# One transfer for ids and bounds, and the last quarter of the second layer's filters issued with the two quarters before it

## The reference

```python
e = stack([tbl_f[ids[:, f]] for f in range(32)], axis=1)          # b, 32, d

prev, outs = e, []
for W in (filter_0, filter_1):                                    # (1024, 128), (4096, 128)
    z = einsum('bhd,bmd->bhmd', e, prev)                          # every field times every map
    cur = relu(einsum('bpd,pn->bnd', z.reshape(b, h*m, d), W))
    outs.append(cur)
    prev = cur
z = concat(outs, axis=1).sum(-1)                                  # b, 256

h = relu(concat([z, dense_ctx], 1) @ W_top1 + b_top1)             # 512
h = relu(h @ W_top2 + b_top2)                                     # 256
y = h @ W_top3
```

## Time and profile before

| | |
|---|---|
| median of 3 runs | 844.33 us (843.94 to 844.5) |
| the profiled execution | 844.57 us |
| its span | 842.8 us |
| TensorE busy | 833.8 us, 99% of the span |
| VectorE, ScalarE, GpSimd busy | 803.8, 782.7, 726.4 us |
| granted TensorE clock | full in all but the very last slices |
| chain of work that ended last | TensorE 94% |

### The profile page before, as it was taken

How to read it: one execution, slowest core, us unless ns; L and a number is a source line. 1 busy time by engine, 2 the same in 40 slices (tenths; PEclk the granted TensorE clock), 3 DMA queues, 4 the chain that set the end, 5 groups by cost and what they waited for, 6 DMA issues and landing times.

```text
span 842.8 us, 17221 instructions
## 1 busy us (share of the span) xinstructions
PE 833.8 (99%) x3595; PEld 670.1 (80%) x3595; DVE 803.8 (95%) x877; ACT 782.7 (93%) x2779; POOL 726.4 (86%) x550
## 2 busy tenths in 40 slices
PE   8999999999999999999999999999999999999998
PEld 6687888888888888888888888888888888888777
DVE  7689999999999999999999999999999999999996
ACT  4799999999999999999999999999999999999984
POOL 5798888999888999888899888899888799988871
PEclk9999999999999999999999999999999999999999
DMA  4551233331232332132232123332123233112000
GB/s 147 166 155 40 56 83 81 83 84 51 43 85 78 82 85 67 29 82 78 83 84 78 30 69 79 83 83 84 41 53 82 79 84 84 47 48 76 1 13 1
DMA packets 62245, 60.17 MB, mean 71 GB/s; under 512 B 26347, under 2 KB 37227, under 8 KB 62222
## 3 DMA queue, kind: packets, MB, share of 16 engines
q1 hardware_dynamic: 58126, 57.80, 23.2%
q0 software_dynamic: 4096, 2.11, 3.3%
HBM read 55.51 MB, written 4.31 MB: 71 GB/s over the span
## 4 chain that ended last, share of the span: by engine, by line
PE 94%; DVE 2%; DMA 1%; POOL 1%; issue 1%; SPq 0%; ACT 0%; DVEq 0%
PE ps_y L895 27%; PE ps_y L903 27%; PE ps_y L896 27%; PE ps_c L868 3%; PE ps_c L878 3%; PE ps_c L877 2%; PE ps_c L876 2%; POOL gat L447 1%; DVE csum L737 1%; PE ps_c L874 1%; DVE prod L724 1%; DMA prod<-w 1%; DMA gat<-table,rows 0%; PE ps_y L999 0%; POOL w_lo L454 0%
## 5 line engine op out<-in xcount | busy, mean ns | idle before, releaser
L559 ACT ACTIVATE prod<-ps_y,es 128x128 f32<-128x128 f32 x2560 | 719.6, 490 | 37.3 <-PE ps_y L903 33.2
L737 DVE TENSOR_REDUCE csum<-prod 128x64 f32<-128x1664 f32 (+2 forms) x256 | 478.8, 1871 | 0.4 <-POOL prod L436 0.2
L895 PE MATMUL ps_y<-w_hi,c_both 128*128 128x512 f32 x1024 | 415.4, 406 | 2.9 <-POOL w_lo L454 2.1
L903 PE MATMUL ps_y<-w_hi,c_both 128*128 128x512 f32 x1024 | 399.6, 390 | 0.0
L896 PE MATMUL ps_y<-w_lo,c_both 128*128 128x512 f32 x1024 | 399.4, 390 | 0.0
L724 DVE TENSOR_TENSOR prod<-ps_y,es 128x512 f32<-128x512 f32 x384 | 256.3, 681 | 23.3 <-PE ps_y L903 17.0
L436 POOL TENSOR_TENSOR prod<-prod 128x768 f32<-128x768 f32 (+1 forms) x128 | 240.4, 1878 | 36.1 <-ACT prod L559 28.1
L895 PEld LDWEIGHTS ps_y<-w_hi,c_both 128*128 128x128 f32 x1024 | 192.4, 188 | 55.3 <-issue 11.5
L896 PEld LDWEIGHTS ps_y<-w_lo,c_both 128*128 128x128 f32 x1024 | 192.4, 188 | 48.2 <-issue 8.2
L903 PEld LDWEIGHTS ps_y<-w_hi,c_both 128*128 128x128 f32 x1024 | 192.2, 188 | 41.9
L426 POOL TENSOR_TENSOR z<-first,second 128x512 f32<-128x512 f32 x155 | 198.1, 1296 | 25.0 <-PE ps_c L874 24.9
(11 more groups left out here) (119 smaller groups left out, 290.0 us busy)
## 6 DMA issues: line engine op xcount, KB each, us to landing
second<-et_scratch SPq DMA_DIRECT2D x155, 256.0 KB, 3.6
first<-et_scratch SPq DMA_DIRECT2D x31, 256.0 KB, 3.3
et_scratch<-gat SPq DMA_DIRECT2D x62, 64.0 KB
prod<-w SPq DMA_DIRECT2D x4, 512.0 KB
h_scratch<-h_sums SPq DMA_DIRECT2D x120, 2.0 KB
gat<-table,rows_now POOLq DMA_INDIRECT x116
wt_sb<-wt SPq DMA_DIRECT2D x2, 512.0 KB
rows_now<-rows SPq DMA_DIRECT2D x30, 2.0 KB, 1.8
```

The lines of the kernel that those rows point to most:

```text
L559: last = nc.scalar.activation(prod[:, buffer_of(g, u), h // 2, :, h % 2], ps_y[:, bank_of(g, u, k), j * N:(j + 1) * N], ACT.Copy, scale=es ...
L737: nc.vector.tensor_reduce(csum[:, g.r, maps, u], prod[:, buffer_of(g, u), fields_folded(g, u) // 2:F // 2, maps, :].rearrange("p a n t -> ...
L895: nc.tensor.matmul(out, hi, w_hi, start=True, stop=False)
L903: nc.tensor.matmul(out, lo, w_hi, start=False, stop=True).then_inc(y_ready, 1)
```

## The change

Ids and bounds come in one array of 128 by 131 words (bounds as the bits of float32, read through a view), so one transfer takes the place of two, and VectorE waits for one. The three `sem_inc` of SyncE go behind quarter 0. Quarter 3 is issued with quarters 1 and 2, after the gathers of group 0, and no longer between `send` and `fetch`. ScalarE rounds bank 6 before bank (0, 1) instead of before (0, 3), and with it the z of the other tiles; bank 7 stays before (0, 3).

```diff
-        ids_sb = sb("ids_sb", [P, TILES], I32)
+        ids_and_bounds_sb = sb("ids_and_bounds_sb", [P, TILES + 3], I32)
-        bounds_sb = sb("bounds_sb", [P, 3])
+        ids_sb = ids_and_bounds_sb[:, 0:TILES]
+        bounds_sb = ids_and_bounds_sb[:, TILES:TILES + 3].bitcast(F32)
...
         def _(sp):
-            for s in range(SLOTS):
-                sp.sem_inc(h1_written[s], 16 * BT)
-            sp.dma_start(ids_sb[:, :], ids).then_inc(ids_in, 16)
-            sp.dma_start(bounds_sb[:, :], bounds).then_inc(ids_in, 16)
+            sp.dma_start(ids_and_bounds_sb[:, :], ids_and_bounds).then_inc(ids_in, 16)
...
             filters(0)
+            for s in range(SLOTS):
+                sp.sem_inc(h1_written[s], 16 * BT)
             sp.wait_ge(gathered[0], 16 * TG)
-            for n in range(1, W1_LOADS - 1):
+            for n in range(1, W1_LOADS):
                 filters(n)
...
             send(Group(0, 1))
-            filters(W1_LOADS - 1)
             fetch(Group(0, 1))
...
-                        if number == 0 and (u, k) == (0, 3):
+                        if number == 0 and (u, k) == (0, 1):
+                            round_w1((6,))
                             act.wait_ge(z_ready, KP)
                             round_z(slice(1, TG), z_hi_ready, SPLIT)
-                            round_w1((6, 7))
+                        if number == 0 and (u, k) == (0, 3):
+                            round_w1((7,))
...
-            dve.wait_ge(ids_in, 32)
+            dve.wait_ge(ids_in, 16)
```

More of the change, by code:

```diff
@@ L112, with tower @@
 LAST = Group((GROUPS - 1) // SLOTS, (GROUPS - 1) % SLOTS)
-def tower(nc, ids, bounds, copy_of, ones_of_b, picks, table, dense_x, dense_w, w0a, w0b, w1, wt1, wt2, bt2, wt3, y):
+def tower(nc, ids_and_bounds, copy_of, ones_of_b, picks, table, dense_x, dense_w, w0a, w0b, w1, wt1, wt2, bt2, wt3, y):
     ctx = ExitStack()
@@ L1114 @@
     arrays = {
-        "ids": np.ascontiguousarray(x["ids"].reshape(GROUPS, BT, TG, F).transpose(1, 3, 0, 2).reshape(P, TILES)),
-        "bounds": np.tile(np.stack([bases + counts - 1, counts, bases], 1).astype(np.float32), (BT, 1)),
+        "ids_and_bounds": np.concatenate([
+            x["ids"].reshape(GROUPS, BT, TG, F).transpose(1, 3, 0, 2).reshape(P, TILES).astype(np.int32),
+            np.tile(np.stack([bases + counts - 1, counts, bases], 1).astype(np.float32), (BT, 1)).view(np.int32)], 1),
         "copy_of": np.tile(np.array([[0, 0], [1, 0], [0, -1], [0, 0]], np.float32), (F, 1)),
```

## The result

The changed kernel takes 846.11 us (median of 21 runs, 844.34 to 847.56), the kernel before 844.3 us (median of 21, 843.71 to 846.41). The ratio is 1.0017, 95% interval 1.0011 to 1.0022, so 0.9 to 1.9 us more (1.8 by the medians). The forecast, 841.7, had been 2.6 us less. The profiled execution took 847.05 us, its span is 845.2.

What follows compares the result with a forecast made beforehand. TensorE, busy throughout from 42.1 to 796.65 us, was taken as the bound, so only the start could gain: 844.57 - 0.4 - 2.3 = 841.9 us profiled, 841.6 for the median, stated as 841.7; range 840.9 to 843.3.

Steps and rivals of the forecast that it cites:

- Bound and transfers: TensorE busy throughout from 42.1 to 796.65 us; joined ids and bounds land 0.31 us sooner, the early fourth quarter by 18.1.
- head: Launch start up to the first rectification: joined transfer 0.31 and moved increments 0.1 us, together 0.4 us gained (0.1 to 0.5).
- the 15.2: Sign of a wrong forecast: ScalarE's rounding of bank 2 starting later than 15.2 us.
- A: Rival: three quarters share the DMA engines, quarter 1 lands 1.1 us later; the launch takes 842.7 us; chance 0.11.
- C: Rival: quarter 1 comes only with the last of all three quarters, 3.3 us late; 844.9 us, slower; chance 0.05.
- `fetch`: Start of fetch, which waits for group 1's gathers: forecast at 22 us (21.2 to 23.5).
- z of group 1: GpSimd's products of group 1: chunk 0 ready at 27.8 us, wanted by TensorE at 29.5, a cover of 1.7 us.
- B: Rival: late cover fails, fetch after 23.8 us or GpSimd makes a fold late; price up to 1.5, 843.1 us; chance 0.07.
- D: Rival: only the earlier start gains, because bank 7's rest on GpSimd is late after all; 843.9 us; chance 0.07.
- ScalarE and GpSimd: ScalarE doesn't wait for the fourth quarter; GpSimd's rests of banks 6 and 7 end at 22.9 and 24.15 us.
- gain of 2.3: TensorE enters bank (0, 6) at 23.46 us without waiting and starts (0, 7) at 24.3 instead of 26.62 us.
- the stretch: TensorE from first pass of bank (0, 2) to that of (1, 0): 8.47 us before; forecast 2.3 us less.

## Why the prediction was wrong

- **Bound and transfers: right; head: right in the first cast.** From bank (1, 0) to L869 TensorE took 4.78 us, as before. The head's 0.4 was 0.49 in the first pair of traces; that the rectification starts earlier by as much in a typical launch isn't shown, as it moves by 1.3 us between traces. ScalarE's rounding that waits for quarter 1 came 4.48 behind the spread (10.36 to 14.84), before 4.38. In the ten traces with the early load this was 4.05 to 4.48 nine times and 5.01 once (in the changed kernel's second profile, past the 15.2 that the prediction named as a sign of A), in the three without it 4.05 to 4.45. So A and C aren't what made the loss; something like A may be at work in single launches. `fetch` at 21.88 (forecast 22); z of group 1 at 26.50 (26.5), no wait before L869 (L868 before): B and D are out. The writes of `send` began at 17.88 instead of 17.08 (17.65 to 19.20 in the ten traces with the early load, 16.95 to 17.08 in the three without), and cost nothing. That agrees with the rule of the Trainium skill on semaphore writes ("DMA: Bandwidth & Descriptors", section "Queues, rings and completion order").
- **ScalarE and GpSimd: right** to 0.3 us.
- **The step that failed** is TensorE's: "It goes from (0, 5) into (0, 6) at 23.46 with no wait", resting on "Nothing that TensorE needs before 23.46 comes later". The list behind it held ScalarE's and GpSimd's instructions, and VectorE's none. What came later was VectorE's z_lo, for which TensorE stood 2.58 us before bank (0, 5). In the kernel before VectorE was idle for 2.36 us, most of the time of GpSimd's rests:

```profile
25.84 0.56 DVE L698 SCALAR_TENSOR_TENSOR c_both<-ps_c,c_both 128x384 fp32r<-128x384 f32 x1 [2.36 <-ACT c_both L530]
```

That idle time was the cover under which two engines did not meet. Moved 2.75 us forward, the rests lay beside two VectorE instructions of the same kind. Instead of a gain of 2.3 the stretch lost 1.83. The difference, 4.13, is the gap of 2.58 (the hold was 2.9, 3.62 - 0.69, and TensorE had some slack) and 1.55 of half clock in the profiled launch. The prediction's sum has neither term: both stood at nothing.
- **Is the rest of the sum right?** Nearly. With the hold off VectorE and GpSimd's rests kept (six rests waited for), 842.58 was measured and a stretch of 6.71, where 841.7 and 8.47 - 2.3 = 6.17 had been forecast: GpSimd starts 0.31 behind its last gather, and its pair takes 2.78 and not 2.51. The 841.83 of the kernel with all rests on VectorE lies close to the forecast by luck: there two rests take 1.29.
- **A page could have told it.** The Trainium skill, "SBUF — State Buffer", section "Who interferes with whom", says that a VectorE instruction with two SBUF inputs contends with a GpSimd instruction that reads SBUF, for a port pair they share. The runs agree: two SBUF inputs held, 3.62, 2.42, 1.62, 1.70; one input from PSUM beside the same GpSimd work, 0.69 and 0.56. I weighed a rule on transfers and not this one. That a port is what they share is the page's reason; the runs show only who is held, and beside which operands.
- **What stays open.** Why, in the changed kernel, VectorE's one instruction let both of GpSimd's pass, while in two other kernels they took turns; what moves the start by up to 1.3 us between executions; and what decides, behind a gap of 2.6 to 2.9 us, whether the clock falls.

## What to carry to other kernels

When work is moved in time, list what every engine does at its new place, and compare operands: VectorE with two SBUF operands and GpSimd reading SBUF held one another wherever they met in the start of these kernels, and the loser may be the one on the path. A hold of this kind shows as one instruction several times as long as its twins, without any wait; look for the maximum beside the mean. A missing wait can cost more than a wait: here one semaphore that held the side engine back by 0.2 or 0.7 us made a slower kernel faster than the original.

## What the runs showed that I had not expected

- In these traces the order of release goes with who holds whom, and the order of the records doesn't: VectorE's instruction starts in the trace at 20.65, GpSimd's at 21.21, and VectorE's is held; with GpSimd's released only near 20.8 it isn't. The same page of the Trainium skill ("SBUF — State Buffer") says in "Who interferes with whom" that issue order decides. Its section "SBUF: two separate sides" says that whoever starts first keeps the pair; that does not fit the starts that the trace shows here, and the measurement decides.
- GpSimd's gathers did not hold VectorE: the rest of bank 4 at 19.45 took 0.68 beside a gather.
- TensorE kept its full clock through gaps of 1.74, 1.34 and 1.19 us in the profiled launches and lost it in three of four with gaps of 2.58 to 2.91; with ten idle matmuls in the gap it kept it.
- With 512 KB more in flight, the first of the loads under way came no later in nine of ten traces, and 0.6 us later in one.
